# The byte offsets of the on-chip buffers in a one-core attention and feed-forward kernel

## What is computed

```python
# x: (32, 256, 128); memory_keys, memory_values: (1, 4096, 128); NH = 1, H = 128
q = x @ Wq.T + bq
scores = q @ memory_keys.T / sqrt(128)
probs = softmax(scores)                       # over the 4096 slots
attn = (probs @ memory_values) @ Wo.T + bo
x = layernorm(x + attn)
h = silu((x @ w1.T) * s1) * ((x @ w2.T) * s2) # 128 -> 512
h = gelu((h @ h1.T) * s_h1)                   # 512 -> 512
h = gelu((h @ h2.T) * s_h2)                   # 512 -> 512
out = layernorm(x + (h @ w3.T) * s3)          # 512 -> 128
```

## Time and profile before

| | us |
|---|---|
| median of 3 runs | 1117.59 |
| lowest and highest | 1116.77, 1117.89 |
| the profiled execution's own time | 1117.46 |
| its span, first to last instruction | 1115.5 |

### The profile page before, as it was taken

The page is one execution under the profiler, slowest core; times in us unless marked ns, Lnnn a source line. Parts: engine busy times, 40 slices in busy tenths (PEclk is TensorE's granted clock), DMA queues, the critical chain, the costliest instruction groups (busy, mean ns, idle before and its releaser), DMA issues.

```text
span 1115.5 us, 20017 instructions
## 1 busy us (share of the span) xinstructions
PE 1079.3 (97%) x5324; PEld 770.6 (69%) x5324; DVE 972.2 (87%) x1806; ACT 903.1 (81%) x1609; POOL 643.0 (58%) x617
## 2 busy tenths in 40 slices
PE   6899999999999999999999999979999999999996
PEld 5666666666666666666666666646888888888875
DVE  6999999999999999999999899897888887888884
ACT  6787788878887888888878878788788888888883
POOL 0487888888888888888888888760211211121111
PEclk9999999999999999999999999999999999999998
DMA  6879888988988889888888998891010010011000
GB/s 202 203 185 212 198 201 210 209 200 202 209 203 206 203 207 210 200 202 209 206 203 204 212 200 188 193 255 55 12 46 28 28 56 28 28 35 50 11 13 27
DMA packets 83957, 165.89 MB, mean 149 GB/s; under 512 B 19664, under 2 KB 47824, under 8 KB 83792
## 3 DMA queue, kind: packets, MB, share of 16 engines
q1 hardware_dynamic: 71536, 154.29, 58.7%
q10 hardware_dynamic: 12384, 11.16, 3.5%
HBM read 22.76 MB, written 8.39 MB: 28 GB/s over the span
## 4 chain that ended last, share of the span: by engine, by line
PE 42%; SPq 13%; issue 11%; POOL 10%; ACT 10%; DMA 6%; DVE 5%; ACTq 1%; POOLq 0%; DVEq 0%
PE ring L1090 13%; SPq L380 12%; PE ring L1091 12%; POOL pT L549 10%; DMA slot_p<-rows 6%; ACT rows L629 5%; ACT pT L638 4%; PE o_ps L1017 2%; PE s_ps L1045 2%; PE s_ps L1043 2%; PE s_ps L1044 2%; PE o_ps L1020 2%; PE o_ps L1022 2%; DVE rows L795 2%; DVE rows L828 1%
## 5 line engine op out<-in xcount | busy, mean ns | idle before, releaser
L549 POOL TENSOR_TENSOR pT<-slot_p,pT 128x512 f16<-128x512 f32 x482 | 546.0, 1167 | 124.4 <-ACT pT L638 124.3
L638 ACT ACTIVATE pT<-slot_p 128x512 f16<-128x512 f32 x512 | 296.5, 617 | 73.8 <-DMA slot_p<-rows 68.6
L828 DVE TENSOR_SCALAR_CACHE_REDUCE rows<-s_ps 128x1024 f32<-128x1024 f32 x256 | 309.4, 1209 | 40.5 <-DMA slot_p<-rows 19.9
L795 DVE STREAM_TRANSPOSE rows<-rows 128x1024 f32<-128x1024 f32 x256 | 316.9, 1239 | 5.9 <-issue 4.1
L629 ACT ACTIVATE rows<-rows,bias 128x1024 f32<-128x1024 f32 x256 | 291.6, 1139 | 6.4 <-DVE bias L836 5.9
L1043 PE MATMUL s_ps<-keys,q_buf 128*128 128x512 f32 x512 | 249.2, 487 | 6.8 <-DVE rows L828 3.5
L1017 PE MATMUL o_ps<-pT,v_hi 128*128 128x512 f16 x512 | 197.4, 385 | 13.3 <-POOL pT L549 6.6
L1045 PE MATMUL s_ps<-keys,q_buf 128*128 128x512 f32 x512 | 202.4, 395 | 0.0
L1044 PE MATMUL s_ps<-keys,q_buf 128*128 128x512 f32 x512 | 201.1, 393 | 0.0
L1020 PE MATMUL o_ps<-pT,v_lo 128*128 128x256 f16 x1024 | 196.1, 273 | 0.0
L1022 PE MATMUL o_ps<-pT,v_hi 128*128 128x512 f16 x512 | 194.6, 380 | 0.0
(11 more groups left out here) (110 smaller groups left out, 1329.2 us busy)
## 6 DMA issues: line engine op xcount, KB each, us to landing
slot_p<-rows SPq DMA_DIRECT2D x1024, 128.0 KB, 3.0
x_in<-in_x SPq DMA_DIRECT2D x16, 256.0 KB, 3.4
x_in<-in_xT ACTq DMA_DIRECT2D x30, 128.0 KB, 3.3
out<-y_out SPq DMA_DIRECT2D x15, 256.0 KB, 2.4
o_scratch<-o_sum ACTq DMA_DIRECT2D x29, 128.0 KB, 2.7
o_in<-o_scratch SPq DMA_DIRECT2D x14, 256.0 KB, 3.1
z<-in_w_all ACTq DMA_DIRECT2D x25, 113.0 KB, 2.7
rows<-in_w_all SPq DMA_DIRECT2D x1, 2816.0 KB, 12.1
```

What stands on the lines that cost most here:

```text
L549: nc.gpsimd.tensor_tensor(halves(s % RING, 1), slots_first(pp, s), halves(s % RING, 0), ALU.subtract).then_inc(split, 1)
L638: nc.scalar.activation(halves(s % RING, 0), slots_first(pp, s), ACT.Copy).then_inc(highed, 1)
L795: nc.vector.transpose(row_piece(tile, k), row_piece(tile, k)).then_inc(turned, 1)
L828: nc.vector.tensor_scalar(row_piece(tile, k), s_ps[:, j % 2, :], 1.0, None, ALU.mult, ALU.max, accum_out=part_max[:, tile, k:k + 1]).then_ ...
```

## The change

Only the order of the calls that reserve SBUF changes, and two buffers that nothing uses are added: `align_first`, 128 bytes ahead of `den`, and `align_small`, 56 bytes behind `w_all`. In `RowStage` the buffers whose size is a multiple of 256 come first, then `w_all` (22600 bytes), then all small ones. No instruction is added, removed or moved on any engine: the streams of the two programs agree row by row. Only the byte offsets differ:

| buffers | use | offset mod 256 before | after |
|---|---|---|---|
| `keys` | moving operand of the scores, first layer, `h1` | 128 | 0 |
| `h_hi1`, `h_lo1` | moving operand of `h2` | 64 | 0 |
| `h_hi2`, `h_lo2` | moving operand of `w3` | 64 | 0 |
| `pT`, `v_hi`, `v_lo` | values | 64 | 0 |
| `w_all` | weights | 128 | 0 |
| `q_buf` | weights of the scores | 64 | 0 |
| `rows` | source of the SBUF to SBUF DMAs | 128 | 0 |
| `slot_p` | their destination | 64 | 0 |
| `gate`, `gelu`, `z2T`, `y_out`, `x_in`, `wq` | | 64 | 0 |
| `o_in`, `x_in2`, `xb`, `z1`, `x1` | | 224 | 0 |
| `o_tmp`, `o_sum` | | 32 | 0 |
| `ident`, `den_sum`, `rden` | | 96 | 0 |
| `stats`, `moments`, `rstd`, `scales` and others under 256 bytes | | various | various |

```diff
         self.x1_hi, self.x1_lo = keys[:, 0:BT], keys[:, BT:2 * BT]
-        self.w_all = sb("w_all", [P, CHECK_COLS * CHECKS], FP32R)
-        self.low_max = sb("low_max", [P, 1], FP32)
-        self.bo_all = sb("bo_all", [P, P], FP32)
-        self.scales = sb("scales", [P, 4 * HC + 1], FP32)
-        self.den_sum = sb("den_sum", [P, TILES], FP32)
-        self.rden = sb("rden", [P, TILES], FP32)
-        self.ident = sb("ident", [P, P], FP32)
-        self.minus_half = sb("minus_half", [P, 4], FP32)
-        self.eps = sb("eps", [P, 4], FP32)
-        self.spare = sb("spare", [P, 2], FP32)
-        self.table_room = sb("table_room", [P, 2], FP32)
         self.o_in = sb("o_in", [P, 2, BT], FP32)
         self.x_in = sb("x_in2", [P, 2, 4, P], FP32)
         self.xb = sb("xb", [P, 4, P], FP32)
         self.z1 = sb("z1", [P, 4, P], FP32)
         self.x1 = sb("x1", [P, 4, P], FP32)
+        self.o_tmp = sb("o_tmp", [P, 2 * P], FP32)
+        self.o_sum = sb("o_sum", [P, 2 * P], FP32)
+        self.bo_all = sb("bo_all", [P, P], FP32)
+        self.ident = sb("ident", [P, P], FP32)
+        self.den_sum = sb("den_sum", [P, TILES], FP32)
+        self.rden = sb("rden", [P, TILES], FP32)
+        self.w_all = sb("w_all", [P, CHECK_COLS * CHECKS], FP32R)
+        sb("align_small", [P, 14], FP32)
         self.stats = sb("stats", [P, 2, 4, 6], FP32)
...
-        self.o_tmp = sb("o_tmp", [P, 2 * P], FP32)
-        self.o_sum = sb("o_sum", [P, 2 * P], FP32)
+        self.minus_half = sb("minus_half", [P, 4], FP32)
+        self.eps = sb("eps", [P, 4], FP32)
+        self.scales = sb("scales", [P, 4 * HC + 1], FP32)
...
     with (
+        nc.sbuf_tensor("align_first", [P, 32], FP32),
         nc.sbuf_tensor("den", [P, PIECES * TOKENS // P], FP32) as den,
```

## The result

| | before | after |
|---|---|---|
| median on the same chip, us | 1117.08 (6 runs, 1116.22 to 1117.89) | 1109.91 (6 runs, 1109.24 to 1110.96) |
| ratio | | 0.9936, interval 0.9924 to 0.9949 |
| span of the profiled execution, us | 1115.5 | 1108.2 |

The kernel is 7.2 us faster. The forecast was 14.8 us (1103 us, range 1097 to 1122): the sign and the range hold, the size is half. The range that the forecast gave its own case, 1097 to 1109, does not hold.

The account below looks back on a forecast made before the run. The prediction took PE to bound the feed-forward turns and, alternating with a chain through other engines and DMA landings, the frames. Turns 12.0 plus frames 2.8 made 14.8 us off 1117.46: 1102.7, called 1103, range 1097 to 1122.

Parts of the forecast that it names:

- the part up to ACT's gate: Feed-forward turn, end of `h1` to start of `h2`: 6.2 us not set by PE's speed; faster matmuls there worth nothing.
- the two-frame chain: Attention frames: POOL, SP's 32 issues, two landings, then ACT and POOL through 16 steps; 44.59 us for two frames.
- Matmuls at offset 0: Float32r matmuls on PE: 0.216 us each at offset 0, instead of 0.2333 in `h2` and 0.2267 in `h1`.
- What of it the turn keeps: Feed-forward turn: `h2` 0.54 and `h1` 0.34 us saved, 0.80 counted a turn after a wait; 15 turns, 12.0 us.
- the wait of 0.04: Feed-forward turn: PE would wait 0.04 us for DVE's x1, the reserve of 0.58 being exceeded by 0.62 saved.
- The frames: Attention frames: 0.2 us saved per pair of frames, 14 steady pairs, 2.8 us.
- 5 of 32 steps of PE: Two attention frames: only 5 steps of 32 are PE's, so 5/16 of a frame's 0.62 us is kept.
- DMAs: Landings in the attention frames: taken as 0, since the same packets arrive; bounds 3 us either way over 28 landings.
- DVE, ACT, POOL at 0: Rows of these engines: no change, bounded by 1% either way, some 0.1 us a frame, 3 us.
- (1): Rival, units of 128 bytes: only `h2` gains, 0.2333 to 0.2267; 0.21 us a turn, 3.1 us, 1114; chance 0.12.
- (2): Rival, nothing: offset not the cause, or only together with where other buffers lie; 1117 to 1118 us; chance 0.20.
- (3): Rival, slower: excess grows to 64 columns at offset 0, 0.240 us a matmul; 1140 us; chance 0.13.

Follow-up runs that it names:

- e1: Kernel before with the buffers behind the weights (`h_*`, `slot_p`, `pT`, `q_buf`) moved to 0 mod 256; 1114.86 us, ratio 0.9975 to before.
- e2: Kernel before with only `keys` and `rows` moved from 128 to 0 mod 256; 1120.35 us, ratio 1.0023 to before.
- e8: Kernel before with only `w_all` moved, from 128 to 64 mod 256, where `h_*` stand; 1115.10 us, ratio 0.9981 to before.
- e9: Kernel before with only `h_*` moved, from 64 to 128 mod 256, where `w_all` stands; 1114.09 us, ratio 0.9970 to before.
- e10: Kernel after with `rows` alone put back to 128 mod 256; 1111.61 us, ratio 0.9947 to before.
- e3: Kernel before with the rear buffers (`h_*`, `slot_p`, `pT`, `q_buf`) at 128 mod 256; 1112.03 us, ratio 0.9949 to before.
- e11: Kernel after with `slot_p` alone put back to 64 mod 256; 1112.21 us, ratio 0.9955 to before.

## Why the prediction was right in sign and twice too large

**The bound of the kernel: right.** PE sets the turn apart from the part up to ACT's gate, and the two-frame chain sets every other frame. Both show in what the change could and could not move.

**"Matmuls at offset 0", the term of 12.0 us: the step that failed.** The value taken was 0.216, near the float16 slots; measured was 0.2267 in both layers, the upper end that the prediction named. `h1` gains nothing on its own, and `h2` 0.16 us a turn instead of 0.54. The term measured is 3.3 us. What misled was to read two excesses, 32 and 48 columns, as a law in the *moving operand's* offset. The two layers also differ in how that offset stands to the one of `w_all`, which is 128: equal in `h1`, not in `h2`. That was in the table of offsets and was not weighed; "what differs is the moving operand's offset" left it out. The runs decide it: `e1` (operand to 0, no gain), `e2` (operand to 0, a loss), `e8` (operand left alone, weights moved, the gain is there). That the turn got faster at all is luck: the change put the weights at 0 together with the operands, for a reason that turned out not to count, and `e2` shows that operands at 0 over weights at 128 lose.

**What of it the turn keeps: right in kind.** `h1` and `h2` are kept in full, and what is saved ahead of `h2` turns into a wait for ACT: 0.07 saved, 0.08 waited. The reserve of DVE's rows of x1 was 0.36 us after, so the wait of 0.04 counted there never came.

**The frames, 2.8 us forecast, 3.7 measured: near in size, wrong in cause.** It was to be 5 of 32 steps of PE made faster. PE's steps in the frame did not get faster (2.71 us a group, 22.08 for the frame that it sets alone). The gain is in the term "DMAs", taken as 0 with bounds of 3 us either way and an argument that did not hold: 0.15 us a mean frame over 18 frames, 3.7 us over the stretch of 29 and 3.8 by the ratios of `e9` and the change, a little above the upper bound. The 3% less engine time per DMA is no proof of the estimate that the prediction worked out from the Trainium skill, "DMA: Bandwidth & Descriptors" (How a descriptor splits into AXI transactions), which counts the bytes fetched ahead of an unaligned source. That estimate is 3% for the source alone, and the source alone gave under 1%: 9.23 to 9.19 in `e2`, 8.99 to 8.95 between `e10` and after. So the size agrees, but most of it came with other buffers. The sentence "I take 0, since the same packets arrive" was the mistake: their number stays, the time of each does not. That landings cause the shorter frame rests on the chain: the last landing of a pair came 0.26 us earlier, where two frames lost 0.29, and over the kernels of the table above the frames are the shorter the earlier it comes. What makes the landings shorter is shown only as far as the placement of buffers; which buffer it is stays open. The sum came to half of the forecast with 3.3 us for 12.0 and 3.7 for 2.8, the second for a cause that the forecast had set to nothing.

**DVE, ACT, POOL at 0: right.** In the frames POOL's rest takes 1168 ns before and 1166 after, ACT's rounding 617 and 618, DVE's transpose 1240 and 1239. Rows after, 850 to 1040 us (busy us, mean ns | idle before), beside the earlier trace rows:

```profile
L896 DVE TENSOR_TENSOR h_lo<-gelu,h_hi 128x512 fp32r<-128x512 f32 x68 | 43.2, 688 | 8.4 <-ACT h_hi L720 8.4
...
L883 DVE TENSOR_TENSOR keys<-gate,keys 128x512 fp32r<-128x512 f32 x36 | 24.0, 688 | 5.1 <-ACT keys L699 4.7
```

**The rivals.** (1), units of 128 bytes, gave 0.2267 in both layers, 0.21 us a turn and 3.1 us: its numbers are those measured, its reason is not, since `e1` should have gained by it. With 3.1 from (1) and the upper bound of 3 for the DMAs the sum would have been 1117.46 - 6.1 = 1111.4; both parts were in the prediction, each put behind a likelier one. (2), nothing: the distances do change with the offsets, but its other half, "only together with where else the buffers lie", describes what was found. (3), slower: 0.240 was seen nowhere, but its sign could have come about, by the mechanism of `e2`, had the change moved `keys` and not the weights.

**Open.** Why equal offsets still cost 226.7 ns where float16 takes 0.220 us a slot, and no offset tried goes below. That the reads of weights and moving operand meet in SBUF would fit a dependence on their difference alone; it is argued, not shown. And which buffer other than `rows` and `slot_p` gives most of what the DMAs gain.

## What to carry to other kernels

Two numbers that fit a formula exactly are still two numbers: list everything in which the two cases differ, here the weights' offset too, before one carries it on. For long trains of float32r matmuls give moving operand and weights the same offset mod 256, which one it is being no matter, and judge it by distances between starts, since the durations hide it; a partial alignment can cost time. For DMAs from SBUF to SBUF that set a chain, the placement of buffers is worth a trial, but not of source and destination alone: here most of the gain came with other buffers, and `e3`, with source and destination at 128, had half of it.

## What the runs showed of the hardware that was not expected

- The distance of float32r matmuls (128x512) depends on the difference between the offsets of moving operand and weights: 226.7 ns at 0, 228.9 at 64, 231.3 to 233.3 at the others tried, at a granted clock of 1.00.
- It takes three to ten matmuls of a train to get there. After the transposes the first distances of `h1`, behind the first of all, are 224 to 236 ns at equal offsets too, and the scores, in trains of six, stay at 232 to 234 in before and after alike. So in a short train the placement is worth little, and the first eight of `h1` got faster (1.86 to 1.81) only because `h2` ahead of them had settled.
- A DMA of 128 KB from SBUF to SBUF (32 partitions x 4096 bytes) took 9.23 engine-us before and 8.95 after; with the same source and destination offsets (0 and 64) it took 9.19 in `e2` and 8.98 in `e11`, where other buffers stand elsewhere.
